# Turning the softmax sums on VectorE in 32x32 blocks instead of on TensorE, in one cross-attention and mixture-of-experts kernel

## The reference, cut to what matters

```python
scores = jnp.einsum('bthd,bshd->bhts', q, k) / np.sqrt(HEAD_DIM)
scores = jnp.where(src_mask[:, None, None, :] == 0, -jnp.inf, scores)
attn = jax.nn.softmax(scores, axis=-1)
tgt_update = jnp.einsum('bhts,bshd->bthd', attn, v).reshape(b, t, OUT_SIZE)
cat_tgt = jnp.concatenate([tgt, tgt_update], axis=2)
return jnp.einsum('btf,of->bto', cat_tgt, W_out) + b_out
```

## Time and profile before

| | |
|---|---|
| median of 3 runs | 1054.44 us (1052.57 to 1055.52) |
| the profiled execution | 1049.61 us, of it 1047.5 us span |
| PE, PEld busy | 1003.0 us (96%), 761.4 us (73%) |
| DVE, ACT, POOL busy | 655.4 us (63%), 467.2 us (45%), 389.4 us (37%) |
| granted clock of TensorE, mean | 0.989 of full speed |
| first `attend` burst, last | 59.9 us, 457.1 us |

### The profile page before, as it was taken

How to read it: one execution, slowest core, us unless ns; L and a number is a source line. 1 busy time by engine, 2 the same in 40 slices (tenths; PEclk the granted TensorE clock), 3 DMA queues, 4 the chain that set the end, 5 groups by cost and what they waited for, 6 DMA issues and landing times.

```text
span 1047.5 us, 14744 instructions
## 1 busy us (share of the span) xinstructions
PE 1003.0 (96%) x5070; PEld 761.4 (73%) x5070; DVE 655.4 (63%) x1510; ACT 467.2 (45%) x881; POOL 389.4 (37%) x355
## 2 busy tenths in 40 slices
PE   4889999999999998899999999999999999999998
PEld 3656767676767664567888888888888888888886
DVE  6866767776767577445665566556556556555544
ACT  3447565666565646445424333333333333333322
POOL 2569797879797967345310010010010100100000
PEclk9999999999999997999999999999999999999999
DMA  7543342424242223325333232242341232332230
GB/s 232 131 132 93 101 132 67 128 72 134 70 114 70 65 64 101 81 81 122 95 72 68 52 81 58 54 82 50 63 80 42 71 82 46 74 75 60 67 72 24
DMA packets 84377, 87.87 MB, mean 84 GB/s; under 512 B 13160, under 2 KB 66296, under 8 KB 84304
## 3 DMA queue, kind: packets, MB, share of 16 engines
q1 hardware_dynamic: 82384, 84.85, 32.9%
q10 hardware_dynamic: 1920, 2.10, 0.6%
HBM read 56.99 MB, written 4.46 MB: 59 GB/s over the span
## 4 chain that ended last, share of the span: by engine, by line
PE 89%; DVE 5%; ACT 2%; SPq 1%; issue 1%; POOL 1%; DMA 1%; DVEq 0%; ACTq 0%; POOLq 0%
PE ps L659 49%; PE pst L659 18%; PE ps L765 5%; PE ps L738 5%; PE pst L754 5%; PE ps L665 4%; DVE mx L1196 1%; PE ps L778 1%; SPq L611 1%; SPq L546 1%; ACT e_buf L866 1%; DVE lg L1277 1%; ACT ctx_h L866 0%; DVE wsrc_l L1145 0%; DMA x<-in_x 0%
## 5 line engine op out<-in xcount | busy, mean ns | idle before, releaser
L659 PE MATMUL ps<-x_h,weights 128*128 128x512 f32 x1088 | 365.6, 397 | 2.8 <-DVE sg L1297 2.0
L659 PEld LDWEIGHTS ps<-x_h,weights 128*128 128x128 f32 x1088 | 204.4, 188 | 52.7 <-issue 2.5
L1196 DVE TENSOR_REDUCE mx<-ps 128x1 f32<-128x512 f32 x256 | 173.2, 684 | 95.4 <-PE ps L738 94.8
L659 PE MATMUL ps<-x_l,weights 128*128 128x512 f32 x544 | 214.5, 394 | 0.0
L866 ACT ACTIVATE hh<-qb 128x512 fp32r<-128x512 f32 x136 | 86.0, 632 | 287.7 <-DVE qb L1311 268.2
L659 PE MATMUL pst<-hh,weights 128*128 128x512 f32 x544 | 193.2, 397 | 0.0
L866 ACT ACTIVATE e_buf<-pst 128x512 f32<-128x512 f32 x256 | 147.1, 595 | 100.4 <-PE pst L754 90.5
L1300 DVE TENSOR_TENSOR qb<-ps,sg 128x512 f32<-128x512 f32 x136 | 94.0, 691 | 135.9 <-PE ps L659 132.2
L1316 DVE TENSOR_TENSOR hl<-qb,hh 128x512 fp32r<-128x512 f32 x136 | 94.3, 693 | 92.2 <-ACT hh L866 92.0
L1406 POOL TENSOR_TENSOR e_sums<-e_sums,e_buf 128x1024 f32<-128x1024 f32 x60 | 143.4, 2390 | 8.6 <-ACT e_buf L866 2.5
L1358 POOL TENSOR_SCALAR ve<-mv 128x4 f32<-128x4 f32 x8 | 1.8, 229 | 337.8 <-DVE mv L1238 337.8
(11 more groups left out here) (154 smaller groups left out, 1360.7 us busy)
## 6 DMA issues: line engine op xcount, KB each, us to landing
cb<-combine_scratch SPq DMA_DIRECT2D x128, 256.0 KB, 4.7
q_stack<-q_h SPq DMA_DIRECT2D x128, 64.0 KB, 2.0
k_stack<-k_h SPq DMA_DIRECT2D x124, 64.0 KB, 2.0
ctx_raw<-in_ctxT SPq DMA_DIRECT2D x7, 1024.0 KB, 5.3
q_stack<-q_l SPq DMA_DIRECT2D x64, 64.0 KB, 2.0
out_x<-ob SPq DMA_DIRECT2D x16, 256.0 KB, 2.1
k_stack<-k_l SPq DMA_DIRECT2D x62, 64.0 KB, 2.0
x<-in_x SPq DMA_DIRECT2D x7, 512.0 KB, 6.8
```

The lines of the kernel that those rows point to most:

```text
L659: ins = engine.matmul(dst, lhsT, rhs, start=start and n == 0, stop=stop and n == len(terms) - 1)
L1196: engine.tensor_reduce(MX[:, g % 2, h // 2, h % 2, q:q + 1], bank(step), AX.X, ALU.max).then_inc(sem("max"), 1)
```

## The change

`out_o`, `turn_s` and `turn_r` are gone, and with them their banks in `RING3`. A new step `sums_t` on DVE turns the sums in blocks of 32x32 straight from PSUM into `SS`: within each block the 32 equal rows of a head become 32 equal columns, so one column of each block holds 32 tokens' sums. `recip` takes that column of the 16 blocks. `spread`, now on DVE, turns the reciprocals back with a second block transpose whose input repeats each value 32 times. `norm_u` multiplies the output in PSUM (`OP`) by `SS` directly. `attend` of the next group waits for `norm_u` where it waited for ACT's copy of `OP`.

```diff
                 elif kind == "attend":
                     if part == 0 and g > 0:
-                        pe.wait_ge(sem("o_sb"), g)
+                        pe.wait_ge(sem("u_norm"), g)
-                elif kind == "turn_s":
-                    turns([(ps[:, 128 * q:128 * q + 128], SS[:, 128 * q:128 * q + 128]) for q in range(4)], sem("s_turned"))
-                elif kind == "turn_r":
-                    turns([(ps[:, 128 * q:128 * q + 128], SS[:, 128 * q:128 * q + 128]) for q in range(4)], sem("r_turned"))
...
-                elif kind == "out_o":
-                    copy(SS[:, :], bank(sums_step(g))).then_inc(sem("s_sb"), 1)
-                    copy(OS[:, :], OP[:, :]).then_inc(sem("o_sb"), 1)
-                elif kind == "spread":
-                    copy(SS[:, :].rearrange("p (q h d) -> p q h d", q=4, h=4),
-                         RU[:, :, :, :].to_broadcast([128, 4, 4, HD])).then_inc(sem("spread"), 1)
...
+                elif kind == "sums_t":
+                    g = step[1]
+                    dve.wait_ge(*burst_done(g, 1))
+                    if g > 0:
+                        dve.wait_ge(sem("u_norm"), g)
+                    engine.transpose(SS[:, :], bank(sums_step(g))).then_inc(sem("sums_t"), 1)
                 elif kind == "recip":
-                    engine.reciprocal(RU[:, :, :, :], bank(("turn_s", g)).rearrange("p (q h d) -> p q h d", q=4, h=4)[:, :, :, 0:1]
+                    engine.reciprocal(RU[:, :, :], SS[:, :].rearrange("p (c r) -> p c r", r=HD)[:, :, 0:1]).then_inc(
+                elif kind == "spread":
+                    g = step[1]
+                    dve.wait_ge(sem("recip"), g + 1)
+                    engine.transpose(SS[:, :].rearrange("p (c r) -> p c r", r=HD),
+                                     RU[:, :, :].to_broadcast([128, S // HD, HD])).then_inc(sem("spread"), 1)
                 elif kind == "norm_u":
-                    engine.tensor_tensor(OS[:, :], bank(("turn_r", g)), OS[:, :], ALU.mult).then_inc(sem("u_norm"), 1)
+                    engine.tensor_tensor(OS[:, :], OP[:, :], SS[:, :], ALU.mult).then_inc(sem("u_norm"), 1)
```

Nearly all times in `attention()` are new as well, most by less than one unit; of that table a few lines:

```diff
-        at(t + 19.7, ("attend", g, 1))
-        at(t + 19.8, ("out_o", g))
-        at(t + 22.2, ("turn_s", g))
+        at(t + 19.1, ("attend", g, 1))
+        at(t + 19.54, ("sums_t", g))
+        at(t + 20.28, ("recip", g))
+        at(t + 21.4, ("spread", g))
+        at(t + 22.1, ("norm_u", g))
...
-    at(-6, ("k", 1, 0))
-    at(-4.9, ("k", 1, 1))
+    at(-9.2, ("k", 1, 0))
+    at(-7.61, ("k", 1, 1))
```

More of the change, by code:

```diff
@@ L126, in attention @@
-    at(-42.4, *first)
+        at(t - 0.82, ("turn_x", b, 1))
+        at(t - 1.11, ("hi_x", b, 1))
+        at(t - -0.12, ("lo_x", b, 1))
+    for i, s in enumerate([("first_loads",), ("ones",), *chain("ln1", N_FIRST1 + 4, 0)]):
+        at(-60 + 0.05 * i, s)
+    at(-50.0, ("wt_hi",))
+    at(-49.5, ("wt_lo",))
+    at(-49.0, ("ctx", 0, 0))
+    at(-46.93, ("ctx", 0, 1))
+    at(-48.0, ("turn_x", 0, 0))
+    at(-47.5, ("hi_x", 0, 0))
+    at(-47.0, ("turn_x", 0, 1))
+    at(-46.5, ("hi_x", 0, 1))
@@ new lines, in attention @@
+    at(-46.46, ("lo_x", 0, 0))
+    at(-45.5, ("lo_x", 0, 1))
+    at(-45.0, ("ctx", 0, 2))
+    at(-44.5, ("ctx", 0, 3))
+    at(-42.74, ("ws_hi", 0))
+    at(-43.5, ("q", 0))
+    at(-44.9, ("ws_lo", 0))
+    at(-42.5, ("out_q", 0))
+    at(-42.0, ("hi_q", 0))
+    at(-41.5, ("load_ctx", 1))
+    at(-41.0, ("k", 0, 0))
+    at(-40.5, ("k", 0, 1))
+    at(-40.0, ("mask_bias",))
+    at(-39.5, ("ws_hi", 1))
+    at(-39.0, ("hi_k", 0))
+    at(-38.5, ("ws_lo", 1))
+    at(-38.0, ("lo_k", 0))
+    at(-37.87, ("bias_row", 0))
@@ L127, in attention @@
+    at(-37.0, ("stack", 0, 0))
+    at(-36.5, ("stack", 0, 1))
+    at(-36.0, ("stack", 0, 2))
+    at(-35.5, ("stack", 0, 3))
+    at(-36.63, ("wo",))
+    at(-38.12, ("q", 1))
+    at(-33.2, ("bv",))
+    at(-33.5, ("v", 0, 0, 0))
+    at(-33.0, ("v", 0, 0, 1))
+    at(-32.5, ("out_q", 1))
+    at(-32.0, ("bo",))
+    at(-31.44, ("out_v", 0, 0))
+    at(-31.0, ("bias_row", 1))
     for i, s in enumerate(chain("ln1", N_LN1, 1)):
-        at(-26.2 if i < 30 else -14.8 + 0.25 * (i - 30), s)
-    at(-14, ("v", 0, 1, 0))
+        at(-30.68 if i < 30 else -15.51 + 0.3 * (i - 30), s)
@@ L141, in attention @@
+    at(-3.17, ("y", 0, 0, 1))
+    at(0.1, ("out_y", 0, 0, 1))
+    at(-9.2, ("k", 1, 0))
+    at(-7.61, ("k", 1, 1))
     at(-7.2, ("hi_q", 1), ("x_bo", 1))
-    at(-5.2, ("hi_k", 1))
-    at(-4.1, ("lo_k", 1))
+    at(-5.21, ("hi_k", 1))
+    at(-5.05, ("lo_k", 1))
     for h, t in enumerate((-2, -1, 0, 1)):
         at(t, ("stack", 1, h))
-    for j in range(16 * NG):
-        at(j - MAX_LEAD, ("max", j // 16, j // 4 % 4, j % 4))
+    for g in range(NG):
+        for n in range(16):
+            when = -13.81 + 1.0 * n if g == 0 else -14.0 + 0.95 * n if g < NG - 1 else -14.1 + 1.02 * n
+            at(16 * g + when, ("max", g, n // 4, n % 4))
@@ L218, in attention @@
     at(t + 26.6, ("gate_up", 5), ("load_c", 5 + NC))
-    for n, when in enumerate((3.6, 7.2, 13, 16.2, 25.3, 26.6)):
-        at(t + when + 0.5, ("silu", n))
-        at(t + when + 0.6, ("unit", n))
-        at(t + when + 2.4, ("hi_h", n))
-        at(t + when + 2.5, ("lo_h", n))
+    for n in range(FIRST_UNITS):
+        at(t + (4.16, 8.12, 13.09, 16.2, 24.91, 26.69)[n], ("silu", n))
+        at(t + (3.11, 8.04, 13.6, 16.8, 25.42, 27.2)[n], ("unit", n))
+        at(t + (4.91, 9.6, 15, 18.6, 27.22, 29.0)[n], ("hi_h", n))
+        at(t + (4.9, 9.7, 15.5, 18.7, 27.32, 29.1)[n], ("lo_h", n))
     at(t + 16.8, ("down", 0))
```

145 lines of the change are left out of this document (57 added, 88 removed).

## The result

The changed kernel takes 1037.61 us (median of 4 runs, 1036.58 to 1040.31), the kernel before on the same chip 1053.51 us: a ratio of 0.985, with a 95% interval of 0.983 to 0.988, or 15.9 us less. The profiled execution took 1037.45 us against the 1049.61 of the one before, 12.2 us less.

What follows compares the result with a forecast made beforehand. PE was taken as the bound, 275.05 of 280 us busy in the attention middle. Terms -14.1 + 1.6 - 3.0 - 1.4 = -16.9 us take the profiled 1049.61 to 1032.7, a median of 1037.5 us; range 1028 to 1047.

Steps and rivals of the forecast that it cites:

- The turns, -14.1: On PE, 32 turns of four 128x128 transposes go, each costing 0.44 us on PE's path: -14.1 us.
- three signs that would make the forecast wrong: New PE idle time behind DVE's reduces; `spread` above 1 us beside POOL's additions; time gained between 390 and 425 us.
- The other moved steps ... I take them as nothing: Remaining re-timed steps of the new order move by a fraction of a unit; costed at nothing.
- The blocks on DVE, 0.70 us each and +1.6 in all: Two block transposes a group on DVE, 1.40 us; 0.1 us a group reaches PE through late `max` banks: +1.6 us.
- The wait that is added: Next `attend` waits for `norm_u` on DVE instead of ACT's copy; over 6 us of slack, so no cost.
- The copies that left ACT, costed at nothing: Three copies a group leave ACT, which had 106 us free of 280; costed at nothing.
- The exponential behind `ctx_h`, -3.0: An exponential now precedes `ctx_h` on ACT, so PE's 0.76 us `scores` wait shrinks by over half, six times: -3.0 us.
- The start, -1.4: At the start, `k` of group 1 now precedes batch 0's second `y` step, which took 1.44 us: -1.4 us.
- The better case: New order closes PE's gaps and slow clock between 392 and 424 us: 9 us more, 1028.5 us; chance 0.16.
- DVE did not set the pace: Rival: transposes do not fit between DVE's reduces and delay PE through late `max` banks: 1062.7 us; chance 0.07.
- The second transpose did not queue behind POOL: Rival: `spread` on DVE waits for POOL's additions, 15.5 us in 16 groups, landing at `max`: 1053 us; chance 0.04.
- The freed time is eaten: Rival: PE's freed turn time becomes idle time waiting for DVE and ACT: 1052 us or so; chance 0.03.

Runs made afterwards that it cites:

- the row copy early: The changed kernel with only `neg` (ACT's copy of the negated maxima and its DMA into `q_stack`) back at 4.9 units of lead instead of 4.25: 1019.32 us, ratio 0.968.

## Why the prediction was right, and where it was not

The time was right to 0.1 us, and that is luck: most of the -14.1 us of the turns was to come from the middle, which gave nothing, and the late stretch and the start gave 13.3 us instead of little. The text named three signs that would make the forecast wrong; the third, "the time is right but comes from the stretch between 390 and 425 us", is nearly what happened (bursts 26 to 29, 384.7 to 432.1 us before, alone gained 11.5). Also, the sum of -16.9 us was meant for the profiled execution, which gained 12.2; the rest of the agreement lies in the distance from the profiled execution to the median, 4.8 us before and 0.2 after.

**The turns, -14.1: the price right, and given back.** 0.43 us a turn was measured on its own. But in the middle nothing of it was left after the change. With the row copy early, two groups of the middle are 2.57 us shorter than before: four turns are 1.76 of them, the shorter wait behind `ctx_h` 0.43, and the remaining 0.4 stand in no row of waits.

**"The other moved steps ... I take them as nothing": the step that failed.** One of them, `neg`, moved by 0.65 units. Together with the loads that then went out ahead of its DMA it cost about 18 us (1037.61 against 1019.32). The reason given, that no row shows a wait of PE that they address, looks at gains only. A moved step can also create a wait, and to see that one has to ask of each what it issues and who waits for the landing. "No DMA and no DMA queue is changed by the division itself" was true and beside the point, for the order changed which DMA goes first.

**The blocks on DVE, 0.70 us each and +1.6 in all.** Size right: 0.715 and 0.702. Without the late DMA PE waits for `max` reduces 4.7 us in the whole run, so +1.6 can stand; with 22.6 us more the rest is 9 us, so it would not stand much more. DVE's wait for `max` fell by 30.6 us where 20 was foretold.

**The wait that is added.** The kernel before makes PE wait for the division in three places: `turn_s` for `s_sb`, `turn_r` for `spread`, `attend` for `o_sb`; the first two went with the turns. The prediction gave `norm_u` over 6 us of slack from its new time of 22.1, and none of the changed kernel's waits names it. In the old order, at 25.3, it is waited for. So part of the new order belongs to the division: the earlier times of `recip`, `spread` and `norm_u` are part of the division's gain (0.995 against 0.986).

**The copies that left ACT, costed at nothing.** In the old order that fits. In the new order PE waits 0.8 us once in two groups for `v_buf` when the copies are there, and not when they are gone. Order and division are worth more together (3.2%) than apart (0.6 and 1.4%).

**The exponential behind `ctx_h`, -3.0.** PE's wait fell from 0.76 to 0.33 us:

```profile
245.31 0.50 PE L785 MATMUL pst<-q_stack,k_stack 98*128 98x512 f32 x1 [0.33 <-ACT e_buf L886]
```

Six times 0.43 is 2.6 us: right.

**The start, -1.4.** Burst 3 came 2.0 us earlier. But the kernels with the same times up to there (the change, its variants with one table or wait changed) have it between 93.00 and 96.82 us, so this term is neither shown nor refuted.

**The rivals.** The better case had the right place and about the right size: 9 us from the stretch after 390, where 11.3 came, 8.0 of them idle time and clock. It failed as a total because it was added to a middle that did not deliver; with the row copy early both come together, and 1019.32 us lies below the range of 1028 to 1047. The 30.1 us between the two profiled executions are then 2.4 at the start, 16.3 in the middle, 10.7 in the late stretch and 0.7 after it. DVE did not set the pace. The second transpose did not queue behind POOL. "The freed time is eaten" was true of the middle, by a DMA and not by the reduces and exponentials that it named.

What stays open: in the late stretch the order alone brings 72.25 us to 66.7, and so does the division alone with its last steps early (at their old times it brings nothing, 72.88); both bring it to 61. Three of the order's tables, put back one at a time, gave up 2.9, 1.5 and 3.5 us of that. Which steps meet there under the old tables was not followed to its end, and how the times of POOL's additions act on the gating chain is open too; nor why old order and old copies on ACT fit together as well as they do.

## What to carry to other kernels

When a change re-times steps by hand, list for each moved step the DMA it issues and what else is on its way to the DMA engines at that moment; a small transfer that an engine waits for belongs ahead of the large prefetches, by a wait if need be. And a total that agrees with a forecast proves little: compare the starts of a recurring mark in both traces, and see whether the time came from where the forecast put it.
